# Softmax probabilities turned in 32x32 blocks by VectorE and regrouped through memory in a fused attention and feed-forward kernel

## What is computed

```python
# x: (4, 256, 256), ctx: (4, 256, 128)
x = x + L0_xattn(layernorm(x), ctx)          # one head
x = L0_ffn(x)                                # 8-bit activations, ternary weights
# L1_xattn on layernorm(x), ctx, 16 query heads, 8 key/value heads of 128
q = (text @ Wq); k = repeat(ctx @ Wk, 2); v = repeat(ctx @ Wv, 2)
attn = softmax(q @ k.T / sqrt(128))          # per head 256 x 256
x = x + (attn @ v).reshape(...) @ Wo
x = x + L1_ffn(layernorm(x))                 # fp8 weights, 768 hidden
```

## Time and profile before

| | us |
|---|---|
| median of 3 runs | 331.1 (331.01 to 331.15) |
| the profiled execution, as timed | 331.73 |
| its span in the trace | 329.9 |
| TensorE busy | 316.4 (96%) |
| VectorE busy | 246.3 (75%) |
| ScalarE busy | 236.9 (72%) |
| GpSimd busy | 205.8 (62%) |
| granted TensorE clock | 1.00 throughout |

### The profile page before, as it was taken

How to read it: one execution, slowest core, us unless ns; L and a number is a source line. 1 busy time by engine, 2 the same in 40 slices (tenths; PEclk the granted TensorE clock), 3 DMA queues, 4 the chain that set the end, 5 groups by cost and what they waited for, 6 DMA issues and landing times.

```text
span 329.9 us, 6627 instructions
## 1 busy us (share of the span) xinstructions
PE 316.4 (96%) x2208; PEld 280.7 (85%) x2208; DVE 246.3 (75%) x724; ACT 236.9 (72%) x545; POOL 205.8 (62%) x316
## 2 busy tenths in 40 slices
PE   4899999999999999899999999999999999999995
PEld 3676676989988988898998999899989999999884
DVE  3898798898887677688777887667547767667583
ACT  2789894786765899766679748656999859664360
POOL 3786353474878748988984778598386632671101
PEclk9999999999999999999999999999999999999999
DMA  7995120040070000021000004000000000000101
GB/s 213 379 374 183 23 91 32 2 144 2 16 128 11 3 0 2 0 51 32 4 0 2 0 2 110 29 0 2 0 2 0 4 0 2 1 2 0 34 32 64
DMA packets 17456, 16.28 MB, mean 49 GB/s; under 512 B 9104, under 2 KB 14864, under 8 KB 17424
## 3 DMA queue, kind: packets, MB, share of 16 engines
q1 hardware_dynamic: 16864, 15.61, 15.7%
q10 hardware_dynamic: 560, 0.26, 0.3%
HBM read 12.85 MB, written 1.05 MB: 42 GB/s over the span
## 4 chain that ended last, share of the span: by engine, by line
PE 61%; ACT 13%; POOL 11%; issue 5%; DMA 5%; DVE 2%; SPq 2%; ACTq 0%; POOLq 0%; DVEq 0%
PE pb L1836 38%; PE pb L2046 6%; PE pb L2095 5%; POOL sm L546 4%; DMA wraw<-in_woutT 3%; PE pb L1911 3%; ACT sm L841 2%; PE pb L2129 2%; PE pb L2003 2%; POOL step L552 1%; PE pb L1950 1%; DMA uqT<-uq 1%; ACT wgv L793 1%; ACT su L820 1%; PE pb L2012 1%
## 5 line engine op out<-in xcount | busy, mean ns | idle before, releaser
L546 POOL TENSOR_SCALAR sm<-sm,srec,mask_all 128x256 f32<-128x256 f32 x128 | 69.6, 556 | 41.2 <-DVE srec L1384 41.2
L841 ACT ACTIVATE sm<-sm,smin 128x256 f32<-128x256 f32 x128 | 63.7, 502 | 10.4 <-DVE smin L1378 10.2
L1378 DVE CUSTOM_DVE_ANT_0 sm<-pb,mask_all 128x256 f32<-128x256 f32 x128 | 48.0, 418 | 14.2 <-PE pb L1836 14.0
L1388 DVE TENSOR_TENSOR pT_lo<-pb,pT_hi 128x512 fp32r<-128x512 f32 x64 | 42.5, 684 | 16.4 <-ACT pT_hi L848 16.1
L848 ACT ACTIVATE pT_hi<-pb 128x512 fp32r<-128x512 f32 x64 | 36.1, 592 | 22.0 <-PE pb L2046 21.9
L1836 PE MATMUL pb<-n_hi,oT_hi 128*128 128x256 f32 x128 | 37.9, 296 | 0.9 <-POOL n_lo L524 0.9
L1836 PE MATMUL pb<-ctx_hi,q_hi 128*128 128x256 f32 x128 | 38.0, 297 | 0.0
L1836 PE MATMUL pb<-xT_hi,m_hi 128*128 128x256 f32 x128 | 36.9, 288 | 0.1
L1836 PE MATMUL pb<-xT_lo,m_hi 128*128 128x256 f32 x128 | 36.2, 283 | 0.0
L1836 PE MATMUL pb<-xT_hi,m_lo 128*128 128x256 f32 x128 | 36.2, 283 | 0.0
L1836 PE MATMUL pb<-n_hi,oT_lo 128*128 128x256 f32 x128 | 36.1, 282 | 0.0
(11 more groups left out here) (189 smaller groups left out, 931.2 us busy)
## 6 DMA issues: line engine op xcount, KB each, us to landing
w_raw<-in_w SPq DMA_DIRECT2D x4, 576.0 KB, 4.5
wraw<-in_wgvT SPq DMA_DIRECT2D x4, 512.0 KB, 7.9
wraw<-in_woutT SPq DMA_DIRECT2D x2, 512.0 KB, 10.4
out<-xb SPq DMA_DIRECT2D x4, 256.0 KB, 2.2
xa<-in_x SPq DMA_DIRECT2D x3, 256.0 KB, 5.5
xb<-in_ctxT SPq DMA_DIRECT2D x2, 256.0 KB, 4.4
stage<-in_wk SPq DMA_DIRECT2D x1, 512.0 KB, 10.4
stage<-in_wv SPq DMA_DIRECT2D x1, 512.0 KB, 12.0
```

The lines of the kernel that those rows point to most:

```text
L546: g.tensor_scalar(sm[:, n % 2, k, :], sm[:, n % 2, k, :], srec[:, n % 2, k:k + 1], mask_all[:, b, S:S + 1], ALU.mult, ALU.mult).then_inc(n ...
L841: a.activation(sm[:, n % 2, k, :], sm[:, n % 2, k, :], ACT.Exp, bias=smin[:, n % 2, k:k + 1], scale=-1.0, accum_out=ssum[:, n % 2, k:k + 1 ...
L1378: v.tensor_tensor_reduce(out=sm[:, n % 2, k, :], in0=bank(passing_bank("s", 2 * n + h))[:, (k % 2) * S:(k % 2 + 1) * S], in1=mask_all[:, b ...
L1388: v.tensor_tensor(pT_lo[:, c, :], bank(passing_bank("pT", SC * n + c)), as_f32(pT_hi[:, c, :]), ALU.subtract).then_inc(pT_lo_done, 1)
```

## The change

Steps 3 to 29 (27 of the 32) get their probabilities turned without TensorE. The chain of such a step n is:

- `normalise`: GpSimd does the second head (k = 2, 3), ScalarE the first (k = 0, 1). This split holds for all 32 steps. The mask column is no longer multiplied in here but at `outputs` and `outputs_low`.
- `turn_blocks` (VectorE): one instruction transposes the 32x32 blocks of the whole `sm[n % 2]`, 1024 columns, into `blocks`, which has one place. Only within blocks; the blocks still stand in the partitions where they were.
- `blocks_written` (SyncE): four DMAs of 128 KB bring them to `block_room` in memory, in runs of 512 bytes, so that a row there is a key.
- `blocks_read` (SyncE): two DMAs of 256 KB bring them back, one for 128 keys each, to `tp`, which has two places.
- `probs` (ScalarE) copies `tp` to `pT_hi`; the low part goes to `tp_lo`, for the first 128 keys by VectorE, for the second by GpSimd (`probs_low`).
- `contexts` (TensorE) reads both through `by_tiles`, since the columns of `tp` are ordered by block.

`probs4` on TensorE stays for steps 0, 1, 2, 30 and 31. All the lists of calls and the table `PASSING` are new; no other work is added or taken away. The core of the diff (the lists and `PASSING` are left out but for a few lines):

```diff
+            tp = tile(unsplit, "tp", [P, 2, SC, 2 * TOK])
+            tp_lo = tile(split, "tp_lo", [P, 2, SC, 2 * TOK], F32R)
+            blocks = tile(turned, "blocks", [P, S // 32, 4, 32])
+        block_room = nc.dram_tensor("block_room", [2 * S, 2 * TOK], F32).ap()
+        FIRST_TURNED, LAST_TURNED = 3, 29
...
+            def blocks_written(n):
+                k = turns_before(n)
+                sp.wait_ge(blocks_done, k + 1)
+                if k >= 2:
+                    sp.wait_ge(blocks_in[0], 16 * (k - 1))
+                    sp.wait_ge(blocks_in[1], 16 * (k - 1))
+                rows = block_room[k % 2 * S:(k % 2 + 1) * S, :].rearrange("(g a) e -> a g e", a=32)
+                for i in range(4):
+                    sp.dma_start(rows[:, :, i * P:(i + 1) * P], blocks[32 * i:32 * (i + 1), :, :, :].rearrange("a g k b -> a g (k b)")).then_inc(blocks_out, 16)
+
+            def blocks_read(n):
...
+                if k >= 2:
+                    sp.wait_ge(oT_ps, n - 1)
+                sp.wait_ge(blocks_out, 64 * (k + 1))
+                for c in range(SC):
+                    if k >= 1:
+                        sp.wait_ge(blocks_in[c], 16 * k)
+                    sp.dma_start(tp[:, k % 2, c, :], block_room[k % 2 * S + c * P:k % 2 * S + (c + 1) * P, :]).then_inc(blocks_in[c], 16)
...
-                for k in (2 * h, 2 * h + 1):
-                    g.tensor_scalar(sm[:, n % 2, k, :], sm[:, n % 2, k, :], srec[:, n % 2, k:k + 1], mask_all[:, b, S:S + 1],
-                                    ALU.mult, ALU.mult).then_inc(norm_done, 1)
+                for k in (2, 3):
+                    g.tensor_scalar(sm[:, n % 2, k, :], sm[:, n % 2, k, :], srec[:, n % 2, k:k + 1], 1.0, ALU.mult, ALU.mult).then_inc(norm_done, 1)
+
+            def probs_low(n, c):
+                pool.wait_ge(pT_hi_done, SC * n + c + 1)
+                z = turned_room(n)
+                g.tensor_tensor(tp_lo[:, z, c, :], tp[:, z, c, :], as_f32(pT_hi[:, c, :]), ALU.subtract).then_inc(pT_lo_pool, 1)
...
+                if by_blocks(n):
+                    act.wait_ge(blocks_in[c], 16 * (turns_before(n) + 1))
+                    whole = tp[:, turned_room(n), c, :]
...
+            def normalise(n):
+                act.wait_ge(srec_done, n + 1)
+                for k in (0, 1):
+                    a.activation(sm[:, n % 2, k, :], sm[:, n % 2, k, :], ACT.Identity, scale=srec[:, n % 2, k:k + 1]).then_inc(norm_act, 1)
...
-                a.activation(oT_hi[:, n % 2, :], bank(passing_bank("ctx", n)), ACT.Copy).then_inc(oT_hi_done, 1)
+                a.activation(oT_hi[:, n % 2, :], bank(passing_bank("ctx", n)), ACT.Identity, scale=some_key(n)).then_inc(oT_hi_done, 1)
...
+            def turn_blocks(n):
+                k = turns_before(n)
+                dve.wait_ge(norm_act, 2 * (n + 1))
+                dve.wait_ge(norm_done, 2 * (n + 1))
+                if k >= 1:
+                    dve.wait_ge(blocks_out, 64 * k)
+                elif n >= 1:
+                    dve.wait_ge(oT_ps, n)
+                v.transpose(blocks[:].rearrange("p g k b -> p k g b"), sm[:, n % 2, :, :].rearrange("p k (g b) -> p k g b", b=32)).then_inc(blocks_done, 1)
...
+                high, low = pT_hi[:, c, :], pT_lo[:, c, :]
+                if by_blocks(n):
+                    high, low = by_tiles(high), by_tiles(tp_lo[:, turned_room(n), c, :])
```

More of the change, by code:

```diff
@@ L993, in _ @@
             exps(7, 0)
             queries(8)
+            normalise(6)
             exps(7, 1)
-            gate_copy(4, 1)
+            probs(4, 0)
+            outputs(3)
+            probs(4, 1)
+            queries(9)
+            normalise(7)
+            outputs(4)
+            probs(5, 0)
+            exps(8, 0)
+            exps(8, 1)
+            probs(5, 1)
+            normalise(8)
+            queries(10)
+            exps(9, 0)
+            exps(9, 1)
             outputs(5)
             probs(6, 0)
+            gate_copy(5, 0)
@@ L1014, in _ @@
[L1014 to L1022 removed]
+            normalise(10)
+            queries(12)
             exps(11, 0)
             exps(11, 1)
[L1025 removed]
+            probs(8, 1)
+            rounded(4)
+            normalise(11)
+            exps(12, 0)
+            queries(13)
+            exps(12, 1)
@@ L1026, in _ @@
+            probs(9, 0)
+            outputs(8)
+            probs(9, 1)
+            gate_copy(6, 0)
+            rounded(5)
+            queries(14)
+            exps(13, 0)
             probs(10, 0)
+            exps(13, 1)
+            normalise(12)
             outputs(9)
             probs(10, 1)
-            queries(13)
-            exps(12, 0)
-            exps(12, 1)
+            gate_copy(6, 1)
+            silu(6)
+            probs(11, 0)
+            queries(15)
+            probs(11, 1)
@@ L1094, in _ @@
             exps(21, 0)
+            outputs(17)
             queries(22)
             exps(21, 1)
-            outputs(19)
+            probs(18, 0)
+            probs(18, 1)
+            rows4(0)
+            queries(23)
+            rows3(3)
+            outputs(18)
+            probs(19, 0)
+            exps(22, 0)
+            normalise(21)
+            probs(19, 1)
+            exps(22, 1)
+            queries(24)
             probs(20, 0)
             probs(20, 1)
-            exps(22, 0)
+            normalise(22)
@@ L1135, in _ @@
-            exps(26, 0)
-            exps(26, 1)
+            normalise(27)
+            fuse_high(0)
+            queries(29)
+            exps(28, 0)
+            exps(28, 1)
             probs(25, 0)
@@ L1676, in _ @@
-            u_max(7)
-            added3(1)
+            second(6)
+            masked(20, 1)
+            added3(1)
+            q_low(21)
+            turn_blocks(19)
+            inverse(20)
+            second(7)
+            probs_low(17, 0)
+            masked(21, 0)
             outputs_low(16)
+            third_stats(3)
+            masked(21, 1)
+            stats4(1)
             eighths(9)
-            probs_low(17, 0)
-            inverse(18)
-            masked(19, 0)
-            probs_low(17, 1)
@@ L1775, in _ @@
+            q_low(30)
+            added3(2)
+            outputs_low(24)
+            eighths(13)
+            turn_blocks(28)
+            masked(30, 0)
+            probs_low(26, 0)
+            fused(2)
+            fused(3)
+            inverse(29)
+            outputs_low(25)
+            turn_blocks(29)
+            outputs_low(26)
+            probs_low(27, 0)
+            masked(30, 1)
+            eighths(14)
+            q_low(31)
+            fuse_low(0)
             probs_low(28, 0)
+            inverse(30)
@@ L1802, in _ @@
             stats4(3)
-            fused(5)
             fuse_low(4)
@@ L2339, in _ @@
+            value_half(6, 1)
+            gate_half(7, 0)
+            gate_half(7, 1)
+            scores(15, 0)
+            rows3(2)
             attn_out(10, 0)
@@ L2416, in _ @@
             queries(23)
-            attn_out(18, 0)
-            probs4(20, 0)
-            probs4(20, 1)
-            attn_out(18, 1)
             scores(22, 0)
             scores(22, 1)
+            rows3(3)
+            contexts(18, 0)
+            contexts(18, 1)
+            queries(24)
+            attn_out(17, 0)
+            attn_out(17, 1)
+            scores(23, 0)
+            scores(23, 1)
+            contexts(19, 0)
+            contexts(19, 1)
+            attn_out(18, 0)
+            scores(24, 0)
```

1544 lines of the change are left out of this document (766 added, 778 removed), and 60 rows, old and new, of the table PASSING.

## The result

The changed kernel takes 328.1 us (median of 20 runs, 326.4 to 330.9), the kernel before 331.5 us in the same comparisons: a ratio of 0.990, with a 95% interval of 0.989 to 0.992. By the ratio it is faster by 3.2 us, where 10.8 were forecast (320.3 us against 331.1). 328.1 lies in the range, in the part that the second rival held ("the gain is eaten"). The ratios leave out one execution of the kernel before, in the comparisons of the first four experiments, which took 391.2 us at a mean granted clock of 0.76.

A forecast was written before the change was run, and what follows sets the result against it. TensorE was taken to bound the attention stage. Its work of 214.5 us at 94% gives 228.2, 11.8 less than 240; 329.9 - 11.8 + 1.0 = 319.1, plus 1.2 makes 320.3 us, range 310 to 337.

The forecast's parts named there:

- the second rival: Attention stage: TensorE only 88 to 91% busy, ScalarE's new waits holding exponentials behind them; 326 to 335 us, chance 0.20.
- the first 60 us: Stretch ahead of the attention stage: new order but the same work, so no change in time.
- TensorE alone bounds the stage: Attention steps, 60 to 300 us: TensorE busy 237.97 of 240, so removed work, 23.5 us, is gained until another engine is late.
- The 94%: Attention stage: TensorE's share with three engines nearly full, from two stretches at 95%; 214.5 / 0.94 = 228.2 us.
- The end: After the attention stage: 1 us more, since four steps in the way must be drained.
- From the span to the median: Whole kernel: 1.2 us added to the span of 319.1 to give 320.3 us.
- ScalarE's work: Attention stage: normalisations, output factors and SBUF copies added, table loads saved; 181.8 us becomes 209.1.
- VectorE's work: Attention stage: 27 low parts given away, 27 transposes and waits for GpSimd added; 179.3 us becomes 200.6.
- GpSimd's work: Attention stage: 64 normalisations less, 27 subtractions more; 169.7 us becomes 168.9, not the bound.
- The strided read of `contexts`: Products of `contexts` read moving columns in runs of 32: taken at no cost, bounds nothing to a doubling.
- The way through memory: Transpose to high part: some 6.9 us, hidden by steps between; loop over `blocks` 4.9 us at best, under 7.2 a step.
- The third rival: Loop over `blocks` longer than a step: slower, some 344 us, 366 at its upper bound; chance 0.12.

The follow-up runs named there:

- the first four experiments: Changed kernel with one write of `blocks` (327.8 us), eight writes (367.0), VectorE's transpose on one 32x32 block (325.5), or ScalarE's normalise on 2 columns (323.4).
- short `pT_hi`, `pT_lo`: Kernel before with six of eight transposes left out in steps 3 to 29, and `pT_hi` and `pT_lo` on 16 columns of 512: 321.2 us.
- short normalise too: Kernel before, six transposes fewer, `pT_hi` and `pT_lo` on 16 columns of 512, and GpSimd's normalise on 16 of 256, steps 3 to 29: 317.4 us.
- three cuts: Changed kernel with one write of `blocks` for four, VectorE's transpose on 32 of 1024 columns and ScalarE's normalise on 2 of 256: 320.1 us.
- GpSimd's normalise too: Changed kernel with one write of `blocks`, VectorE's transpose on one block, and normalise on 2 columns on both ScalarE and GpSimd: 320.0 us.
- a product between: Changed kernel with `contexts(n, 1)` one call later on TensorE in 23 of 27 steps, another product between its halves: 341.5 us.

## Why the prediction was wrong, step by step

One table draws the stage together. TensorE's work in it is the counted one (237.97 us before, less what was taken out, and 4.5 us more where the first 60 us had left them over); the length is 240 us, or 235 for the changed kernel, less the difference of the profiled spans (329.9 and 324.5).

| kernel | span | TensorE's work | stage | share |
|---|---|---|---|---|
| before | 329.9 | 238.0 | 240.0 | 99% |
| before, two transposes fewer | 327.0 | 232.6 | 237.1 | 98% |
| before, six fewer | 322.5 | 221.8 | 232.6 | 95% |
| the same, short `pT_hi`, `pT_lo` | 318.9 | 221.8 | 229.0 | 97% |
| the same, short normalise too | 315.5 | 221.8 | 225.6 | 98% |
| changed | 324.5 | 219.0 | 235.0 | 93% |
| changed, three cuts | 319.3 | 219.0 | 229.8 | 95% |
| changed, GpSimd's normalise too | 316.5 | 219.0 | 227.0 | 96% |

The spans are those of one run each. By the medians the last two rows are equal, at 96%, the changed kernel's is 92.5%, and the others move by half a percent at most.

Two steps of the prediction failed. In the reasoning, it is that TensorE alone bounds the stage and the others' slack is room. In the sum, it is the first 60 us, a term put at nothing, which measured 4.8 us; the share of TensorE, which carried the reasoning, was off by only 2.0 us.

**TensorE alone bounds the stage; what is taken off it is gained one for one.** This step failed. It read 237.97 of 240 as the one limit and the others' quarter of slack as room. The runs with fewer transposes show 0.65 us per microsecond for the first 5 and 0.3 for the next 11, with no engine near its limit. While TensorE is behind it hardly waits (7.1 us of its weight loads in 240); as soon as it gets ahead, it meets the chain of the others (22.4 us in 235).

**The 94%.** The number was near, in part by luck, and its reason was half wrong. It came from two stretches of 20 us of a kernel in which nothing had been taken off TensorE. It measures 93% of the counted work, so 219.0 / 0.932 = 235 in place of 219.0 / 0.94 = 233: 2.0 us. But I took it as the price of three nearly full engines. The kernel before with six transposes fewer has 95% without any, so most of it is the price of a leaner TensorE in a fixed order. Only the step down to 93% from the 95 or 96% of the three cuts is that of the time that the new instructions take on ScalarE and VectorE, 8 us of the median.

**The first 60 us.** Taken as unchanged "in a new order but with the same work". They hold 4.5 us less of TensorE, at 94% 4.8 us: the largest term of the miss. The test stood in the prediction (a first 60 us that moved by more than 3). The loss lies between 20 and 60 us. TensorE's waits of the changed kernel from 20 to 50 us, where the kernel before has three, of 1.3 us in all:

```profile
PE pb L2090 <- ACT aT L882: 1.8, 1, 1.8
PE pb L2090 <- issue: 1.5, 1, 1.5
PE pb L2075 <- ACT aT L882: 1.4, 2, 0.7
PE pb L2149 <- DMA stage<-in_wv: 1.0, 1, 1.0
```

**The end.** Forecast 1 us more; the last part is 29.5 us long where it was 29.9. That is 1.4 us better than forecast. With this the span is closed: 319.1 + 4.8 + 2.0 - 1.4 = 324.5. (It closes by construction, since the stage's share is its measured length; the terms say where the time went, not why.)

**From the span to the median.** I added 1.2 us: 325.7. The median is 328.1, 2.4 us more: the profiled run is the fastest of 20, 1.7 us under the median, where the profiled run before was 0.6 over its own. 5.4 + 2.4 = 7.8 us is the whole miss. The last section shows what differs from run to run.

**ScalarE's work.** Forecast 209.1 us, found 208.6, of which some 2 were left over by the first 60 us (43.63 for 45.73); over the whole run it grew by 25.7 where 27.3 were forecast. Two normalisations in a row take 0.90 us, so 0.4 from start to start, as taken from the earlier trace rows. `outputs` with a factor took 680 ns (685 taken) and the copies from SBUF 621 (627).

**VectorE's work.** Forecast 200.6, found 200.2. The transpose takes 1241 ns where the reduction that stood for it showed 1.21 us. The low parts took 860 ns on the mean (648 at least, 693 median, 1735 at worst), 0.18 us over the quiet 683 where I had put 0.26. All thirteen over 0.70 us overlap an instruction of GpSimd that had started first, and the three longest (1393, 1640 and 1735 ns) start 0.1 to 0.4 us behind a subtraction of GpSimd; the six that meet none take 683 to 693 ns, and eight that meet one take no longer. The long cases agree with what the Trainium skill, "SBUF — State Buffer", "Who interferes with whom", says of the two engines; at its worst it would have been 35 us, and it was 27 x 0.18 = 4.8. The other page cited, "Vector Engine (DVE) Microarchitecture Reference" of the Trainium skill, section 3.8, gave one element per cycle and lane; the transpose's 1024 elements per lane in 1241 ns are 1.2 ns each, as for the reduction of 1024, so it is in keeping with it.

**GpSimd's work.** Forecast 168.9; found 171.6, the subtraction being 1351 ns and not 1289. I called it no bound. It is none, but its low part is the largest single wait of TensorE.

**The strided read of `contexts`** costs next to nothing, as taken. The three products start 0.23 and 0.25 us apart, against 0.23 in the earlier trace rows; the medians over the trace are 0.235 to 0.238 against 0.231 to 0.233, 0.7 us over all 162:

```profile
200.11 0.40 PE L2015 MATMUL pb<-pT_hi,cr_hi 128*128 128x512 f32 x1
200.34 0.40 PE L2015 MATMUL pb<-tp_lo,cr_hi 128*128 128x512 f32 x1
200.59 0.40 PE L2015 MATMUL pb<-pT_hi,cr_lo 128*128 128x512 f32 x1
```

**The way through memory.** Latency hidden, as forecast (one write in place of four: nothing). The loop is 1.24 + 1.86 + 2.5 = 5.6 us, not 4.9 (a write takes 0.46 us to issue), under 6.9 a step, and waits 2.3 us in all. The third rival was sized right: its cliff appears with four more writes, when the loop passes the step: 8.2 us and 367 us, where the rival had 366 for 8.5.

**The signs.** The transpose (1.24 us), `normalise` (0.40) and the landing (2.5 at the median, 4.1 at worst) came out as named. TensorE's busy time in the stage didn't: 225.1, or 220.6 without the 4.5 left over, for "near 214". Nor did ScalarE's share, 89% for "above 90%". And the first 60 us moved by more than 3, which was named as breaking the sum.

**The rivals.** The second came true in its time and not in its place: its reason was ScalarE's queue, whose cut gives 4.6 us, while the first 60 us and the chain as such weigh more. The fourth, VectorE as the bound, failed with the transpose's duration.

Open is the early part: which place of the new lists costs the 4.5 us, and whether an order exists that keeps them. The one try with the lists of before didn't find it. Nor was a new order made for the changed loads; the runs with moved work show only that lists not made for it lose, all but the one with one tile on ScalarE. Open is also how much of each loss is the load of an engine and how much the length of the chain: every cut that shortened an instruction took from both.

## What to carry to other kernels

A busy share is no measure of slack. Before work is taken off the bounding engine, take a part of it off without giving it to anybody and look at the time: here one such run says that 16 us are worth 7, before any new code is written. Where each engine follows a fixed list, forecast the time as work divided by a share, and read that share from a run in which the bounding engine is already ahead. A wait at the top of the table is not a price: covering it by moving one call a step gave back 3.6 us of that wait and cost 13. And runs whose clock differs are to be compared with care.

## What the runs showed of the chip that I had not expected

**TensorE's granted clock falls after short gaps in some runs and not in others.** The stretches 30 to 34 and 34 to 38 us, first in the changed kernel, then with the three cuts, whose work is the same up to there:

```profile
30.00:34.00 4.00, 2.11 (x15) 1.34 (x14) 3.86 (x14) 3.98 (x6) 3.56 (x6) 1.00 0.44 131
34.00:38.00 4.00, 4.00 (x18) 1.99 (x17) 3.65 (x15) 3.52 (x6) 1.88 (x3) 1.00 0.11 22
```
```profile
30.00:34.00 4.00, 2.12 (x13) 1.17 (x12) 3.86 (x14) 3.98 (x6) 3.56 (x6) 0.90 0.38 131
34.00:38.00 4.00, 4.00 (x12) 1.83 (x11) 2.33 (x9) 2.65 (x4) 1.83 (x3) 0.68 0.12 25
```

In both TensorE was busy for 2.1 of the first 4 us. In one it stays at 2.4 GHz; in the other the mean falls to 0.90 and then 0.68, so it spent part of the time at 1.2 GHz, and 12 products end where 18 did. The kernel before is busy for 3.3 of the first 4 us there, and its runs vary by 1.6 us, the changed kernel's by 4.5. Of its 20 runs the eight with a mean clock of 1.000 have a median of 327.4 us (six lie between 326.4 and 327.8), and the six at 0.995 and below lie between 328.1 and 330.9. So the clock accounts for 0.7 of the 1.7 us between the profiled run and the median; the other 1.0 is that the profiled run was fast even among those at 1.000. That the gaps cause the fall is argued, not shown.

Within the runs of one kernel, 0.001 less of mean clock goes with 0.3 us more (one slope fitted to the 90 runs of the changed kernel and the sixteen experiments). With this estimate the means can be brought to a clock of 1.000: the changed kernel 327.6 us, one write in place of four 326.0, early order as before 327.6, all low parts on VectorE 340.6, a product between 338.0, the three cuts 319.8, and with GpSimd's cut too 318.4. The early order is then level with the changed kernel, of the 18 us of the low parts 5 are the clock's, and GpSimd's cut is worth 1.4 us where the medians show none.

**The loop through memory has a sharp edge.** Next to nothing for a shorter way, 39 us for four more writes, some 2 us of issuing.
